# Channel attention on TensorE: the attention weights turned and multiplied with the final weights, then one product over the values

## Chip, cores and metric

The kernel runs on one core of a Trainium2 chip. The metric is the device time of one execution in microseconds; three runs of the kernel before gave a median of 491.94 us (491.89 to 494.11).

## The reference

The input is a batch of 32 images of 96 channels and 16 x 16 pixels. Two layers follow each other: a shifted-window attention with its MLP (layer 0), and a channel attention (layer 1). The change lies in layer 1, whose end is:

```python
Q = _proj(xn, wq_p, bq_p, wq_d, bq_d)
K = _proj(xn, wk_p, bk_p, wk_d, bk_d)
V = _proj(xn, wv_p, bv_p, wv_d, bv_d)
logits = jnp.einsum('bhnc,bhnd->bhcd', K, Q) / alpha[None, :, None, None]
attn = jax.nn.softmax(logits, axis=-1)
out = jnp.einsum('bhnc,bhcd->bhnd', V, attn)
...
return jnp.einsum('bcij,oc->boij', out, w_f) + b_f[None, :, None, None] + xn
```

There are 8 heads of 12 channels each. A head's attention weights are a 12 x 12 matrix, so for one image the weights of all heads are one block matrix over the channels. The output of an image is the final weights times these weights times the values: a chain of three matrices, whose product may be formed from either end.

## The kernel before

Two functions share the work: `window_attention` does layer 0's attention image by image, and `mlp_and_channels` (from L917) does layer 0's MLP, in groups of tokens, and then layer 1, image by image. All matrices are float32. A float32 product appears in the trace as two passes (x2), a transpose by the identity as one.

The last part, from about 340 us to the end, is a loop over images. Its order is written out by hand, one list of calls for each engine (`step`, called by `lap_loop`, L906), and engines meet at semaphores alone. In step t TensorE (L1645) does, in this order:

1. `turn_keys(t)` (L1562): four transposes of queries and keys of image t.
2. `attend(t - 1)` (L1582): attention weights of image t - 1 over its values, 256 columns, into `ps_av`.
3. `queries_and_keys(t + 1)` and, later, `values(t + 1)` (both through `convolve`, L1535): the convolutions, as 24 and 12 small products on tiles of the array 32 columns wide.
4. `gram(t)` (L1570), between the two: 16 products of 12 columns on tiles 32 columns wide.
5. `finalise(t - 1)` (L1589): the final weights over `av_sb`, 256 columns, into `ps_y`.

ScalarE (L1253) copies results from PSUM to SBUF in order: `copy_av(t - 1)` (L1209), `copy_qk(t + 1)` (L1195), the exponent of image t's logits (L1205), a small copy of moments, `copy_v(t + 1)` (L1200) and `pad_x`. VectorE (L1447) copies the turned tokens, normalises a later image, subtracts the peak from the logits, divides by the row sum (`divide`, L1376, which writes `attn`), and adds the residual (`finish`, L1391). SyncE and GpSimd issue the transfers that stack the taps of a later image, and SyncE stores the result.

Values have two buffers, `v_sb[:, par, :]`. `SLOTS` is 4 and is the number of buffers of a padded image; `ROUNDS` is 2, the halves into which the 8 heads are split. `need` is a wait that is left out where its count is not positive. The first copies of `lap_loop`'s body and the last eight are unrolled, the rest is a loop with a register.

Of the kernel before, what the change touches and what calls it, by code (L numbers as in the profile page):

```python
# [20 lines left out]
B, C, H, W = 32, 96, 16, 16  # L21
N = H * W
# [33 lines left out]
def need(engine, semaphore, count):  # L56

    if isinstance(count, int) and count <= 0:
        return
    engine.wait_ge(semaphore, count)  # L60
# [836 lines left out]
SLOTS = 4  # L897
# [19 lines left out]
def mlp_and_channels(nc, ctx, sem, stream, ident, average, w, m, s2, stack_ones, out):  # L917
# [5 lines left out]
    def sb(name, shape, dt=F32):  # L923
        return ctx.enter_context(nc.sbuf_tensor(name, shape, dt))
# [20 lines left out]
    x_pad = sb("x_pad", [C, SLOTS, PADW, PADW])  # L945
    x_stack = sb("x_stack", [128, SLOTS, TILE_HEADS, ROWS])
    qk_sb = sb("qk_sb", [128, ROUNDS, N])
    v_sb = sb("v_sb", [128, 2, N])
    tokens = sb("tokens", [128, 2, ROUNDS, 128])
    logits = sb("logits", [128, ROUNDS, HC])  # L950
    peak = sb("peak3", [128, ROUNDS])
    row_sum = sb("row_sum", [128, ROUNDS])
    recip_sum = sb("recip_sum", [128, ROUNDS])
    attn = sb("attn", [128, ROUNDS, 64])
    av_sb = sb("av_sb", [128, N])
    y_sb = sb("y_sb", [C, 2, N])
    padded_x = nc.dram_tensor("padded_x", (B, C, PADW * PADW), F32, kind="Internal").ap()

# [2 lines left out]
    ps_early = banks[:, 4:8, :]  # L961
    ps_qk = banks[:, 0:2, 0:N]
    ps_v = banks[:, 2, 0:N]
    ps_av = banks[:, 3, 0:N]
    ps_gram = banks[:, 4, 0:ROUNDS * HC].rearrange("p (r d) -> p r d", r=ROUNDS)
    ps_y = banks[0:C, 5, 0:N]
    ps_moments = banks[0:C, 6, 0:2 * B].rearrange("p (t e) -> p t e", e=2)
# [25 lines left out]
    s3 = {n: sem(n + "_3") for n in (  # L993
        "moment_ready", "gained", "normed", "x_padded", "qk_ready", "v_ready", "qk_copied", "v_copied", "tok_ready",
        "tok_copied", "gram_ready", "peak_ready", "shifted", "exp_ready", "sum_ready", "recip_ready",
        "attn_ready", "av_ready", "av_copied", "final_ready", "y_ready")}
    ZEROED = 5
    ONES = 2 * ROUNDS
    OWN = ROUNDS * TILE_HEADS
# [151 lines left out]
    @block.scalar  # L1151
    def _(act):
        def gelu(g, part):
            act.wait_ge(s["hidden_ready"], g * HT + part + 1)
            need(act, s["y_ready"], (g - 1) * SLICES)
            home = ps_early if (g, part) == (0, 1) else ps_hidden
            for r in range(QUARTERS):
                nc.scalar.activation(hidden[:, g % 2, r, part, :], home[:, r, :], ACT.Gelu,  # L1158
                                     bias=fc1_b[:, part:part + 1]).then_inc(s["gelu_ready"], 1)

        def deviation(b):

            first, last = BATCHES[b]
            act.wait_ge(moments_set, MOMENT_OPS * b + 5)
            nc.scalar.activation(log_var[:, first:last], variance[:, first:last], ACT.Ln, scale=0.5,
                                 bias=eps[:, 0:1]).then_inc(log_set, 1)
            act.wait_ge(log_set, b + 1)
            nc.scalar.activation(moments[:, first:last, 0], log_var[:, first:last], ACT.Exp, scale=-0.5).then_inc(rstd_set, 1)

        def await_batch(b):  # L1170

            act.wait_ge(moments_set, MOMENT_OPS * (b + 1))
            act.wait_ge(rstd_set, b + 1)

        def copy_weights(place, kind):

            act.wait_ge(weights_turned, SIDE * (place + 1) + place // 2)
            for half in range(ROUNDS):
                rows, heads = slice(64 * half, 64 * half + STACK), slice(half * HALF_C, (half + 1) * HALF_C)
                at = HC * (half if kind else 1 - half)  # L1180
                nc.scalar.copy(conv_w[rows, kind // 2, :, :, at:at + HC],
                               ps_weights[rows, :, heads].rearrange("p j (h c) -> p j h c", c=HC)).then_inc(weights_copied, 1)

        def take_moment(t, par):

            need(act, s3["normed"], t - 1)
            nc.scalar.copy(moment[:, par, :], moments[:, bass.ds(t, 1), :].rearrange("p a b -> p (a b)")).then_inc(s3["moment_ready"], 1)

        def pad_x(t, lap, slot):

            act.wait_ge(s3["normed"], t + 1)
            act.wait_ge(written[slot], lap * 16)
            nc.scalar.copy(x_pad[:, slot, 1:H + 1, 1:W + 1], grid(stream[:, bass.ds(t * N, N)])).then_inc(s3["x_padded"], 1)

        def copy_qk(t):  # L1195
            act.wait_ge(s3["qk_ready"], t + 1)
            need(act, s3["tok_ready"], t)
            nc.scalar.copy(qk_sb[:, :, :], ps_qk).then_inc(s3["qk_copied"], 1)  # L1198

        def copy_v(t, par):  # L1200
            act.wait_ge(s3["v_ready"], t + 1)
            need(act, s3["av_ready"], t - 1)
            nc.scalar.copy(v_sb[:, par, :], ps_v).then_inc(s3["v_copied"], 1)

        def exponent(t):  # L1205
            act.wait_ge(s3["shifted"], t + 1)
            nc.scalar.activation(logits[:, :, :], logits[:, :, :], ACT.Exp).then_inc(s3["exp_ready"], 1)

        def copy_av(t):  # L1209
            act.wait_ge(s3["av_ready"], t + 1)  # L1210
            need(act, s3["final_ready"], t)
            nc.scalar.copy(av_sb[:, :], ps_av).then_inc(s3["av_copied"], 1)  # L1212

        for g in range(GROUPS - 1):
            later = g > 0
            gelu(g, 0)
            if later:
                for r in range(2):
                    copy_tokens(nc, act, m, s, (g + 1) * QUARTERS + r, tokens_home(r))
            gelu(g, 1)  # L1220
            if later:
                for r in range(2, QUARTERS):
                    copy_tokens(nc, act, m, s, (g + 1) * QUARTERS + r, tokens_home(r))
                nc.scalar.preload_act_table_set("natural_log_exp_and_others")
                token_deviation(nc, act, m, s, g + 1)
                nc.scalar.preload_act_table_set("gelu_and_others")
            gelu(g, 2)
        act.wait_ge(zeroed, ZEROED)
        gelu(3, 0)
        nc.scalar.preload_act_table_set("natural_log_exp_and_others")  # L1230
        deviation(0)
        nc.scalar.preload_act_table_set("gelu_and_others")
        gelu(3, 1)
        copy_weights(0, 1)
        copy_weights(1, 0)
        gelu(3, 2)
        copy_weights(2, 2)
        nc.scalar.copy(final_w[:, :], ps_final).then_inc(weights_copied, 1)
        nc.scalar.preload_act_table_set("natural_log_exp_and_others")
        copy_qk(0)  # L1240
        await_batch(0)
        take_moment(AHEAD, 0)
        copy_v(0, 0)
        deviation(1)

        copy_qk(1)
        exponent(0)
        take_moment(AHEAD + 1, 1)
        copy_v(1, 1)
        pad_x(AHEAD, 1, AHEAD % SLOTS)  # L1250
        await_batch(1)

        def step(t, lap, slot):  # L1253
            copy_av(t - 1)
            if not past(t + 1):
                copy_qk(t + 1)
            exponent(t)
            if not past(t + AHEAD + 1):
                take_moment(t + AHEAD + 1, (slot + AHEAD + 1) % 2)
            if not past(t + 1):  # L1260
                copy_v(t + 1, 1 - slot % 2)
            if not past(t + AHEAD):
                pad_x(t + AHEAD, lap + (slot + AHEAD) // SLOTS, (slot + AHEAD) % SLOTS)
            if is_image(t, 3):
                deviation(2)
                await_batch(2)

        lap_loop(act, step)
        copy_av(B - 1)

    @block.vector
    def _(dve):
# [103 lines left out]
        def divide(t):  # L1376
# [2 lines left out]
            dve.wait_ge(s3["sum_ready"], t + 1)  # L1379
            nc.vector.reciprocal(recip_sum[:, :], row_sum[:, :]).then_inc(s3["recip_ready"], 1)  # L1380
            dve.wait_ge(s3["recip_ready"], t + 1)
            need(dve, s3["av_ready"], t)
            for r in range(ROUNDS):

                nc.vector.scalar_tensor_tensor(  # L1385
# [85 lines left out]
    def _(pe):  # L1471
# [107 lines left out]
                                              tokens[:, n, r, queries:queries + HC], start=(n == 0), stop=(n == 1))  # L1579
            mm.then_inc(s3["gram_ready"], 1)  # L1580

        def attend(t, par):  # L1582
            pe.wait_ge(s3["attn_ready"], (t + 1) * ROUNDS)
            pe.wait_ge(s3["v_copied"], t + 1)
            need(pe, s3["av_copied"], t)
            nc.tensor.matmul(ps_av, attn[:, :, :].rearrange("p r d -> p (r d)"), v_sb[:, par, :], start=True,  # L1586
                             stop=True).then_inc(s3["av_ready"], 1)

        def finalise(t):  # L1589
            pe.wait_ge(s3["av_copied"], t + 1)  # L1590
            need(pe, s3["y_ready"], t)
            nc.tensor.matmul(ps_y, final_w[:, :], av_sb[:, :], start=True, stop=True).then_inc(s3["final_ready"], 1)  # L1592

        up(0, 0)
        up(0, 1)
# [49 lines left out]
        def step(t, lap, slot):  # L1645
            turn_keys(t)
            if not past(t + 1):
                await_taps(t + 1, lap + (slot + 1) // SLOTS, (slot + 1) % SLOTS)
            attend(t - 1, 1 - slot % 2)
            if not past(t + 1):  # L1650
                queries_and_keys(t + 1, (slot + 1) % SLOTS)
            gram(t)
            if is_image(t, 3):
                average_means(2)
            if not past(t + 1):
                values(t + 1, (slot + 1) % SLOTS)
            finalise(t - 1)
            if is_image(t, 3):
                average_spreads(2)

        lap_loop(pe, step)
        attend(B - 1, 1)
        finalise(B - 1)


# [52 lines left out]
```

## Time and profile before

| | before |
|---|---|
| median of three runs | 491.94 us |
| the profiled execution | 491.68 us |
| its span | 490.0 us |
| what lies around the span | 1.68 us |
| TensorE matmuls busy | 475.3 us (97%) |
| weight loads busy | 308.8 us (63%) |
| VectorE busy | 366.1 us (75%) |
| ScalarE busy | 294.8 us (60%) |
| granted clock of TensorE, mean | 0.996 |

The profile comes from one execution. PE is TensorE's matmuls and PEld its weight loads, which can run beside matmuls; DVE is VectorE, ACT is ScalarE. Matmuls are pipelined and their ends are modelled, so the starts of groups say more than their durations. A row of the timeline joins neighbouring instructions of one line: start, time from the first start to the last end, engine, line, what it writes and reads, shape, count, and in brackets the idle time ahead of it and what ended it.

### The profile page before, as it was taken

To read this page: it belongs to the slowest core of one execution; us is meant where nothing else is said; L and a number is where in the kernel's file an instruction comes from. 1 tells how busy PE (TensorE), PEld (TensorE's weight loads), DVE (VectorE), ACT (ScalarE), POOL (GpSimd) and SP (SyncE) were. 2 spreads that over 40 slices of the span, in tenths; PEclk is the share of its full clock that TensorE was granted. 3 is DMA by queue.
4 is the path that set the end of the run, shared out by engine and by line. 5 is a ranking of instruction groups with operands and counts; after the bars stand their busy time and mean duration, and the time that the engine had idled before them with its cause. 6 is when DMAs were issued, how large, how long until landed. Compare 5 with 4: busy or idle time off the path is not lost. (4 is left out here: it accounts for less than half of the span.)

```text
span 490.0 us, 21340 instructions
## 1 busy us (share of the span) xinstructions
PE 475.3 (97%) x8006; PEld 308.8 (63%) x8006; DVE 366.1 (75%) x1013; ACT 294.8 (60%) x757; POOL 186.0 (38%) x230
## 2 busy tenths in 40 slices
PE   8999999999999999999969999999899999999996
PEld 7777777777777777777844344344566666666663
DVE  1599999999999999999873546654966666666553
ACT  2477877787778778877656747642344344444332
POOL 8634343434344434443333012652232333433300
PEclk9999999999999999999999999999999999999998
DMA  4210111111101110110004543475445444444411
GB/s 79 72 36 18 34 33 46 21 33 33 30 19 32 32 27 21 32 32 1 4 7 98 93 105 89 117 181 131 108 111 131 120 107 132 120 111 125 121 41 33
DMA packets 41963, 33.29 MB, mean 68 GB/s; under 512 B 19456, under 2 KB 37760, under 8 KB 41920
## 3 DMA queue, kind: packets, MB, share of 16 engines
q1 hardware_dynamic: 37952, 26.21, 21.5%
q0 software_dynamic: 3968, 6.51, 5.8%
q8 instruction: 28, 0.46, 0.4%
q14 instruction: 15, 0.12, 0.1%
HBM read 19.25 MB, written 7.13 MB: 54 GB/s over the span
## 5 line engine op out<-in xcount | busy, mean ns | idle before, releaser
L379 POOL TENSOR_TENSOR scores<-scores,peak 128x768 f32<-128x768 f32 x64 | 94.2, 1472 | 129.6 <-DVE peak L548 129.6
L1542 PE MATMUL banks<-x_stack,conv_w 40*32 40x256 f32 (+1 forms) x2304 | 97.0, 380 | 0.0
L1017 POOL DMA_DIRECT2D x_stack<-padded_x x96 | 52.3, 548 | 94.6 <-PE banks L1542 56.4
L442 ACT COPY probs_t<-ps_probs 128x768 f32<-128x768 f32 x64 | 51.1, 798 | 40.3 <-PE ps_probs L704 40.2
L1542 PEld LDWEIGHTS banks<-x_stack,conv_w 40*32 40x32 f32 (+1 forms) x2304 | 51.7, 107 | 26.9 <-issue 11.3
L540 DVE TENSOR_TENSOR scores<-ps_scores,bias 128x768 f32<-128x768 f32 x64 | 61.3, 957 | 5.3 <-PE ps_scores L694 3.5
L548 DVE TENSOR_REDUCE peak<-scores 128x12 f32<-128x768 f32 x64 | 61.0, 953 | 2.4
L717 PE MATMUL ps_out<-v_blocks,probs_t 128*64 128x54 f32 x1536 | 57.2, 224 | 0.6 <-ACT out_t L447 0.6
L717 PEld LDWEIGHTS ps_out<-v_blocks,probs_t 128*64 128x64 f32 x1536 | 50.2, 138 | 11.8 <-issue 11.7
L436 ACT ACTIVATE scores<-scores 128x768 f32<-128x768 f32 x64 | 54.2, 847 | 1.5 <-POOL scores L379 1.5
L704 PE MATMUL ps_probs<-ident,scores 128*128 128x128 f32 x384 | 54.3, 277 | 0.0
L694 PE MATMUL ps_scores<-k_blocks,q_sb 32*64 32x256 f32 x768 | 43.1, 399 | 0.9 <-issue 0.9
L704 PEld LDWEIGHTS ps_probs<-ident,scores 128*128 128x128 f32 x384 | 41.5, 140 | 2.8 <-issue 0.8
L527 DVE SCALAR_TENSOR_TENSOR k_blocks<-ps_scores,b_k,head_mask 96x1024 f32<-96x1024 f32 x32 | 40.5, 1267 | 2.8 <-PE ps_scores L672 2.8
L1198 ACT COPY qk_sb<-banks 128x512 f32<-128x512 f32 x32 | 18.8, 587 | 39.0 <-PE banks L1542 39.0
L1158 ACT ACTIVATE hidden<-banks,fc_b_folded 128x512 f32<-128x512 f32 x48 | 29.0, 688 | 21.8 <-PE banks L1498 21.8
L1498 PE MATMUL banks<-normed,fc_sliced 32*128 32x512 f32 x288 | 34.0, 603 | 4.3 <-PEq L148 3.2
L1509 PE MATMUL banks<-hidden,fc 128*32 128x512 f32 x288 | 33.4, 596 | 0.0
L1371 DVE TENSOR_REDUCE peak<-banks 128x2 f32<-128x24 f32 x32 | 5.8, 183 | 36.3 <-PE banks L1578 36.3
L871 POOL TENSOR_TENSOR scaled<-tokens,rstd 128x384 f32<-128x384 f32 x16 | 12.7, 826 | 47.5 <-ACT rstd L863 42.1
L1212 ACT COPY av_sb<-banks 128x256 f32<-128x256 f32 x32 | 11.9, 372 | 27.2 <-PE banks L1586 27.2
L1498 PEld LDWEIGHTS banks<-normed,fc_sliced 32*128 32x128 f32 x288 | 14.3, 184 | 18.7 <-issue 15.8
(146 smaller groups left out, 809.8 us busy)
## 6 DMA issues: line engine op xcount, KB each, us to landing
x_stack<-padded_x SPq DMA_DIRECT2D x96, 54.0 KB
x_stack<-padded_x POOLq DMA_DIRECT2D x96, 54.0 KB, 2.7
padded_x<-x_pad SPq DMA_DIRECT2D x32, 121.5 KB, 2.5
stream<-y_sliced SPq DMA_DIRECT2D x48, 64.0 KB, 2.8
out<-y_sb SPq DMA_DIRECT2D x32, 96.0 KB, 1.9
x_now<-in_x SPq DMA_DIRECT2D x32, 72.0 KB, 1.8
stream<-in_x SPq DMA_DIRECT2D x32, 72.0 KB, 1.9
x_sliced<-stream SPq DMA_DIRECT2D x36, 64.0 KB, 2.0
```

The lines of the kernel that those rows point to most:

```text
L379: nc.gpsimd.tensor_tensor(sc, sc, peak[:, par, p, :].unsqueeze(2).to_broadcast((128, HEADS, WN)), ALU.subtract).then_inc(s["shifted"], 1)
L436: nc.scalar.activation(scores[:, par, p, :], scores[:, par, p, :], ACT.Exp).then_inc(s["probs_ready"], 1)
L442: nc.scalar.copy(probs_t[:, :], ps_turned).then_inc(s["turned_copied"], 1)
L527: nc.vector.scalar_tensor_tensor(out=k_blocks[:, :, :], in0=ps_k.unsqueeze(1).to_broadcast((C, GROUP, N)), scalar=b_k[:, 0:1], in1=head_ma ...
L540: nc.vector.tensor_tensor(scores[:, par, p, :].rearrange("p (g c) -> p g c", g=NG), ps_scores[:, :, 0:GROUP * WN], bias[:, p, :].rearrange ...
L548: nc.vector.tensor_reduce(peak[:, par, p, :], scores[:, par, p, :].rearrange("p (h m) -> p h m", m=WN), AX_X, ALU.max).then_inc(s["peak_re ...
L694: mm = nc.tensor.matmul(ps_scores[64 * w:64 * w + 64, g, 0:GROUP * WN], q, k, start=True, stop=True, skip_group_check=True)
L704: mm = nc.tensor.transpose(ps_turned[:, q * 128:(q + 1) * 128], scores[:, par, p, q * 128:(q + 1) * 128], ident[:, :])
L717: mm = nc.tensor.matmul(ps_out[64 * top:64 * top + 64, 0, q * 2 * VC:(q + 3) * 2 * VC], probs_t[:, q * 128 + 64 * top:q * 128 + 64 * top + ...
L1017: engine.dma_start(x_stack[64 * half + i * HC:64 * half + (i + 1) * HC, slot, :, :], rows).then_inc(landed[slot], 16)
L1498: mm = nc.tensor.matmul(home[:, r, :], fc1[rows, c, part * 128:(part + 1) * 128], normed[rows, c, :], start=(c == 0), stop=(c == SLICES - 1))
L1542: mm = nc.tensor.matmul(home, conv_w[rows, kind, j, k, :], grid(x_stack[rows, slot, k, :], PADW)[:, :, j:j + W], start=(j == 0), stop=(j = ...
```

## The change

For an image, the attention weights are turned on TensorE (`turn_attn`), copied to SBUF, and multiplied with the final weights (`mix`, 96 columns); the result is copied to SBUF, and one product of it with the values (`finalise`, 256 columns) gives the output. The product of the attention weights with the values, and the copy of it, are left out. The values of an image are now needed until the final product, so they have four buffers. The two small results share PSUM bank 3, where the attention over the values was.

```diff
-    v_sb = sb("v_sb", [128, 2, N])
+    v_sb = sb("v_sb", [128, SLOTS, N])
...
-    av_sb = sb("av_sb", [128, N])
+    attn_t = sb("attn_t", [128, 128])
+    mix_sb = sb("mix_sb", [128, C])
...
-    ps_av = banks[:, 3, 0:N]
+    ps_attn_t = banks[:, 3, 0:128]
+    ps_mix = banks[:, 3, 128:128 + C]
...
-        def copy_v(t, par):
+        def copy_v(t, slot):
             act.wait_ge(s3["v_ready"], t + 1)
-            need(act, s3["av_ready"], t - 1)
-            nc.scalar.copy(v_sb[:, par, :], ps_v).then_inc(s3["v_copied"], 1)
+            need(act, s3["final_ready"], t - SLOTS + 1)
+            nc.scalar.copy(v_sb[:, slot, :], ps_v).then_inc(s3["v_copied"], 1)
...
-        def copy_av(t):
-            act.wait_ge(s3["av_ready"], t + 1)
+        def copy_attn(t):
+            act.wait_ge(s3["attn_turned"], t + 1)
+            need(act, s3["mix_ready"], t)
+            nc.scalar.copy(attn_t[:, :], ps_attn_t).then_inc(s3["attn_copied"], 1)
+
+        def copy_mix(t):
+            act.wait_ge(s3["mix_ready"], t + 1)
             need(act, s3["final_ready"], t)
-            nc.scalar.copy(av_sb[:, :], ps_av).then_inc(s3["av_copied"], 1)
+            nc.scalar.copy(mix_sb[:, :], ps_mix).then_inc(s3["mix_copied"], 1)
...
         def step(t, lap, slot):
-            copy_av(t - 1)
+            copy_attn(t - 1)
+            copy_mix(t - 1)
             if not past(t + 1):
                 copy_qk(t + 1)
...
-            need(dve, s3["av_ready"], t)
+            need(dve, s3["attn_turned"], t)
...
-        def attend(t, par):
+        def turn_attn(t):
             pe.wait_ge(s3["attn_ready"], (t + 1) * ROUNDS)
+            need(pe, s3["mix_copied"], t)
+            nc.tensor.transpose(ps_attn_t, attn[:, :, :].rearrange("p r d -> p (r d)"), ident[:, :]).then_inc(s3["attn_turned"], 1)
+
+        def mix(t):
+            pe.wait_ge(s3["attn_copied"], t + 1)
+            nc.tensor.matmul(ps_mix, attn_t[:, :], final_w[:, :], start=True, stop=True).then_inc(s3["mix_ready"], 1)
+
+        def finalise(t, slot):
+            pe.wait_ge(s3["mix_copied"], t + 1)
             pe.wait_ge(s3["v_copied"], t + 1)
-            need(pe, s3["av_copied"], t)
-            nc.tensor.matmul(ps_av, attn[:, :, :].rearrange("p r d -> p (r d)"), v_sb[:, par, :], start=True,
-                             stop=True).then_inc(s3["av_ready"], 1)
-
-        def finalise(t):
-            pe.wait_ge(s3["av_copied"], t + 1)
             need(pe, s3["y_ready"], t)
-            nc.tensor.matmul(ps_y, final_w[:, :], av_sb[:, :], start=True, stop=True).then_inc(s3["final_ready"], 1)
+            nc.tensor.matmul(ps_y, mix_sb[:, :], v_sb[:, slot, :], start=True, stop=True).then_inc(s3["final_ready"], 1)
...
-            attend(t - 1, 1 - slot % 2)
+            turn_attn(t - 1)
             if not past(t + 1):
                 queries_and_keys(t + 1, (slot + 1) % SLOTS)
+            mix(t - 1)
             gram(t)
...
-            finalise(t - 1)
+            finalise(t - 1, (slot - 1) % SLOTS)
```

The calls after the loop change in the same way: `attend` and `finalise` of the last image become `turn_attn`, `mix` and `finalise`, and `copy_av` becomes `copy_attn` and `copy_mix`.

TensorE's list for one step in the kernel before (the names that end in _3 are semaphores of layer 1; L1542 with x23 or x24 is `queries_and_keys`, with x11 `values`):

```order
L1567 MATMUL banks<-ident,qk_sb 128x128 x3
L1586 MATMUL banks<-v_sb,attn 128x256 [waits attn_ready_3,v_copied_3,qk_copied_3,av_copied_3,stacked_pool3,stacked_sp3]
L1542 MATMUL banks<-x_stack,conv_w 32x256 x24
L1578 MATMUL banks<-tokens 32x12 [waits shifted_3,tok_copied_3]
L1578 MATMUL banks<-tokens 32x12 x15
L1542 MATMUL banks<-x_stack,conv_w 32x256 [waits v_copied_3]
L1542 MATMUL banks<-x_stack,conv_w 32x256 x11
L1592 MATMUL banks<-av_sb,final_w 96x256 [waits y_ready_3,av_copied_3]
```

The same step in the changed kernel (its line numbers are its own: L1594 is `turn_attn`, L1598 `mix`, L1604 `finalise`):

```order
L1576 MATMUL banks<-ident,qk_sb 128x128 x3
L1594 MATMUL banks<-ident,attn 128x128 [waits attn_ready_3,qk_copied_3,mix_copied_3,stacked_pool3,stacked_sp3]
L1551 MATMUL banks<-x_stack,conv_w 32x256 x24
L1598 MATMUL banks<-final_w,attn_t 128x96 [waits attn_copied_3]
L1587 MATMUL banks<-tokens 32x12 [waits shifted_3,tok_copied_3]
L1587 MATMUL banks<-tokens 32x12 x15
L1551 MATMUL banks<-x_stack,conv_w 32x256 [waits v_copied_3]
L1551 MATMUL banks<-x_stack,conv_w 32x256 x11
L1604 MATMUL banks<-v_sb,mix_sb 96x256 [waits y_ready_3,v_copied_3,mix_copied_3]
```

At the place of the product of 256 columns there is now a transpose of 128, and a product of 96 columns stands alone between the convolution of queries and keys and the Gram product.

ScalarE's list for one step in the kernel before:

```order
L1212 COPY av_sb<-banks 128x256 [waits final_ready_3,av_ready_3]
L1198 COPY qk_sb<-banks 128x512 [waits tok_ready_3,qk_ready_3]
L1207 ACTIVATE logits<-logits 128x24 [waits shifted_3]
L1187 COPY moment<-moments 96x2 [waits normed_3]
L1203 COPY v_sb<-banks 128x256 [waits av_ready_3,v_ready_3]
L1193 COPY x_pad<-stream 96x16x16 [waits written2,normed_3]
```

And in the changed kernel:

```order
L1214 COPY attn_t<-banks 128x128 [waits mix_ready_3,attn_turned_3]
L1219 COPY mix_sb<-banks 128x96 [waits final_ready_3,mix_ready_3]
L1200 COPY qk_sb<-banks 128x512 [waits tok_ready_3,qk_ready_3]
L1209 ACTIVATE logits<-logits 128x24 [waits shifted_3]
L1189 COPY moment<-moments 96x2 [waits normed_3]
L1205 COPY v_sb<-banks 128x256 [waits final_ready_3,v_ready_3]
L1195 COPY x_pad<-stream 96x16x16 [waits written2,normed_3]
```

One copy of 256 columns has become two, of 128 and 96; the second waits for the product ahead of the Gram product, and the copy of queries and keys stands behind it.

## Rows read from the trace of the kernel before

**Rows 1.** The head of the page: span, then busy us, share and instructions.

```profile
span 490.0 us, 21340 instructions
PE 475.3 (97%) x8006; PEld 308.8 (63%) x8006; DVE 366.1 (75%) x1013; ACT 294.8 (60%) x757; POOL 186.0 (38%) x230
```

**Rows 2.** Busy time in a 30 us stretch, then granted clock, DMA share, GB/s.

```profile
410.00:440.00 30.00, 30.00 (x717) 18.68 (x706) 19.26 (x67) 13.19 (x41) 9.82 (x18) 1.00 0.45 121
```

**Rows 3.** Timeline of TensorE's matmuls, one image and the next Gram product.

```profile
405.04 0.44 PE L1578 MATMUL banks<-tokens 128*32 128x12 f32 x32
...
405.32 1.51 PE L1542 MATMUL banks<-x_stack,conv_w 104*32 104x256 f32 x24
...
406.75 0.67 PE L1592 MATMUL banks<-av_sb,final_w 128*96 128x256 f32 x2
...
407.26 0.60 PE L1567 MATMUL banks<-ident,qk_sb 128*128 128x128 f32 x4
...
407.70 0.60 PE L1586 MATMUL banks<-v_sb,attn 128*128 128x256 f32 x2
...
408.23 1.53 PE L1542 MATMUL banks<-x_stack,conv_w 40*32 40x256 f32 x48
...
409.68 0.44 PE L1578 MATMUL banks<-tokens 128*32 128x12 f32 x32
```

**Rows 4.** Timeline of the weight loads in the same image.

```profile
405.04 0.35 PEld L1578 LDWEIGHTS banks<-tokens 128*32 128x32 f32 x32 [0.41 <-issue]
...
406.75 0.24 PEld L1592 LDWEIGHTS banks<-av_sb,final_w 128*96 128x96 f32 x2 [0.41 <-issue]
...
407.59 0.30 PEld L1586 LDWEIGHTS banks<-v_sb,attn 128*128 128x128 f32 x2
...
408.23 1.04 PEld L1542 LDWEIGHTS banks<-x_stack,conv_w 40*32 40x32 f32 x48 [0.33 <-issue]
```

**Rows 5.** Views of lines 1586 and 1592: loads, ns min/median/max.

```profile
L1586 PEld LDWEIGHTS banks<-v_sb,attn x64: 186/190/192, 339.8 to 485.1; 128*128 128x128 f32 x64
...
L1592 PEld LDWEIGHTS banks<-av_sb,final_w x64: 159/162/280, 343.6 to 486.3; 128*96 128x96 f32 x64
```

**Rows 6.** Timeline of TensorE at image 3: a small product between two groups.

```profile
353.70 0.36 PE L1518 MATMUL banks<-stats,average 96*96 96x32 f32 x2
353.99 1.50 PE L1542 MATMUL banks<-x_stack,conv_w 104*32 104x256 f32 x24
```

**Rows 7.** Timeline of TensorE at images 2 and 3: the Gram product's wait.

```profile
347.60 0.44 PE L1578 MATMUL banks<-tokens 128*32 128x12 f32 x32 [1.01 <-DVE tokens L1366]
...
353.33 0.44 PE L1578 MATMUL banks<-tokens 128*32 128x12 f32 x32 [1.02 <-DVE tokens L1366]
```

**Rows 8.** Timeline of ScalarE and VectorE in the image of rows 3.

```profile
405.22 0.59 ACT L1198 COPY qk_sb<-banks 128x512 f32<-128x512 f32 x1 [1.15 <-PE banks L1542]
...
406.09 0.22 ACT L1207 ACTIVATE logits<-logits 128x24 f32<-128x24 f32 x1 [0.28 <-DVE logits L1373]
...
406.78 0.45 DVE L1385 SCALAR_TENSOR_TENSOR attn<-logits,recip_sum,own_head 128x48 f32<-128x48 f32 x2
...
408.33 0.37 ACT L1212 COPY av_sb<-banks 128x256 f32<-128x256 f32 x1 [0.79 <-PE banks L1586]
```

**Rows 9.** Timeline of the last image, and busy time and clock near the end.

```profile
482.57 0.37 ACT L1212 COPY av_sb<-banks 128x256 f32<-128x256 f32 x1 [1.10 <-PE banks L1586]
...
482.89 0.44 PE L1578 MATMUL banks<-tokens 128*32 128x12 f32 x32 [0.35 <-DVE tokens L1366]
...
485.01 0.70 PE L1586 MATMUL banks<-v_sb,attn 128*128 128x256 f32 x2 [1.08 <-DVE attn L1385]
485.75 0.37 ACT L1212 COPY av_sb<-banks 128x256 f32<-128x256 f32 x1 [1.68 <-PE banks L1586]
...
486.17 1.17 PE L1592 MATMUL banks<-av_sb,final_w 128*96 128x256 f32 x2 [0.46 <-ACT av_sb L1212]
...
486.00:487.00 1.00, 0.83 (x2) 0.40 (x2) 0.00 (x0) 0.12 (x1) 0.00 (x0) 0.51 0.35 98
```

More of the change, by code:

```diff
@@ L995, in mlp_and_channels @@
         "tok_copied", "gram_ready", "peak_ready", "shifted", "exp_ready", "sum_ready", "recip_ready",
-        "attn_ready", "av_ready", "av_copied", "final_ready", "y_ready")}
+        "attn_ready", "attn_turned", "attn_copied", "mix_ready", "mix_copied", "final_ready", "y_ready")}
     ZEROED = 5
@@ L1260, in step @@
             if not past(t + 1):
-                copy_v(t + 1, 1 - slot % 2)
+                copy_v(t + 1, (slot + 1) % SLOTS)
             if not past(t + AHEAD):
@@ L1268, in _ @@
         lap_loop(act, step)
-        copy_av(B - 1)
+        copy_attn(B - 1)
+        copy_mix(B - 1)
     @block.vector
@@ L1661, in _ @@
         lap_loop(pe, step)
-        attend(B - 1, 1)
-        finalise(B - 1)
+        turn_attn(B - 1)
+        mix(B - 1)
+        finalise(B - 1, (B - 1) % SLOTS)
 _INS = ['x', 'L0_conv_qkv_w', 'L0_conv_qkv_b', 'L0_conv_proj_w', 'L0_conv_proj_b', 'L0_conv_rel_bias',
```

## Prediction, made before the changed kernel ran

> **What bounds the kernel now.** I began with the head of the profile's page: TensorE is busy for 97% of a span of 490.0 us [rows 1]. Such a share can hide slack, because ends of matmuls are modelled, so I asked for the busy times of one stretch in the middle of the channel attention, the stage that the change edits: in 30 us TensorE is busy for all 30.00, VectorE for 19.26 and ScalarE for 13.19 [rows 2]. The timeline of one image then shows TensorE's groups without a hole: Gram product at 405.04, values at 405.32, final weights at 406.75, turns of queries and keys at 407.26, attention over the values at 407.70, convolution of the next queries and keys at 408.23, next Gram product at 409.68 [rows 3]. One image is 4.64 us. So an image here costs what TensorE's groups cost from start to start, and the question is what the new groups cost on that scale.
>
> The starts give four prices. A turn of 128 columns is 0.44 / 4 = **0.11 us** [rows 3], so one pass of 256 columns is about 0.21 and one of 96 columns 0.08. Products run as two passes, since each of them shows as x2. A **load** of a stationary matrix is hidden behind the matmul before it when the array keeps its shape. Where the shape changes it is not: the load queue stands idle for 0.33 or 0.41 us and starts only when the group before is over [rows 4]. The final product shows the price: 0.51 us [rows 3] are two passes (0.43) and one open load of 96 columns, 0.08. Its pair of loads says the same: 0.24 together [rows 4], one lasts 0.16 [rows 5], so the second began 0.08 after the first. For 128 columns it is 0.30 together [rows 4] and 0.19 for one [rows 5], so 0.11. And there is a **tail** where a group hands over to another shape: attention over the values takes 0.53 [rows 3], of which two passes are 0.43, so 0.10 is left.
>
> One row tests these prices. At image 3 a small product of 32 columns with a 96-column load stands between two groups of other shapes and takes 353.99 - 353.70 = 0.29 us [rows 6]. My terms give two loads (2 x 0.08, for a pass of 32 columns, 0.03, is too short to hide the second), 0.03 for the last pass and 0.10 of tail: 0.29.
>
> **The change part by part.**
>
> *Attention over the values goes, the turn comes.* 0.53 is removed at its place. The turn there is one pass of 128 columns with its load hidden, for the turns of queries and keys ahead of it have the same shape: 0.11, and the tail of 0.10. Together 0.21, a gain of 0.32 for an image.
>
> *The mix product comes between queries-and-keys and the Gram product.* Both neighbours have other shapes, so this is a new hand-over in each image. No row has it; I bound it. Open load of 128 columns 0.11; first pass 0.08, behind which the second load (0.11) does not fit, so 0.11; second pass 0.08; tail 0.10: **0.40 us**. Lower end 0.34, if loads cost what 96 columns cost (0.08 + 0.08 + 0.08 + 0.10); upper end 0.48, if passes and loads do not overlap at all (0.22 + 0.16 + 0.10). I take 0.40, since the same working meets the 0.29 of the nearest row [rows 6]. The tails of its neighbours are paid already: queries and keys hand over to another shape before and after.
>
> The Trainium skill, "TensorEngine Tiling (Array Packing)", section Tiling Modes, says that a switch of the tiling mode drains TensorE, which speaks against this change. The trace agrees, with the 0.10 us tail; by that rule the sum is mine, and by a switch that cost nothing at the new place it would be 27 x 0.10 = 2.7 us less.
>
> *The final product* keeps its place and shape (a load of 96 columns, two passes of 256): 0.
>
> So an image costs 0.40 - 0.32 = **+0.08 us** more; with unrounded starts I get 0.07 and use that (ends 0.01 and 0.15).
>
> *How many images pay it.* Images 2 and 3 do not: there the Gram product waits 1.01 and 1.02 us for VectorE's copy of the tokens [rows 7], and TensorE's extra work disappears in that hole. Image 3 also leaves its attention to VectorE. From the step of image 4 to that of image 30 TensorE is the bound, so turn and mix count 27 times, 27 x 0.07 = 1.9 to 2.0 us; image 1 adds 0.07, because VectorE's long chain starts from its Gram product.
>
> *ScalarE.* The one 256-column copy (0.37) becomes one of 128 columns and one of 96. Two of its copies, 0.37 for 256 columns and 0.59 for 512 [rows 8], give 0.16 + 0.00084 a column: 0.26 and 0.24. ScalarE has room for 0.13 more. The order matters, though: the copy of the mix now stands ahead of the copy of queries and keys, and that ahead of the exponent on which the next attention depends. The copy of queries and keys starts 0.18 after TensorE passes on to the Gram product (405.22 against 405.04). With the mix there, a copy may start 0.18 after the Gram product's start, take 0.24, and the next 0.59: over at +1.01. The exponent starts at +1.05 today, held by VectorE [rows 8]. It stays there, so I cost this at nothing; the cover is 0.04 us there and, behind it, the gap between the end of the attention weights (406.78 + 0.45) and the load that waits for them (407.59 [rows 4]), 0.36, or 0.31 after the 0.05 that a release takes at the end of the program (a copy over at 486.12, its reader's load at 486.17 [rows 9]). The copy of the turned weights runs under 1.45 us of convolution and is early. The copy of the mix is over some 1.3 us before the final product.
>
> *Queues and buffers.* SyncE and GpSimd issue the same transfers in the same order. Values stay two images longer in four buffers instead of two; the copy into them waits for a final product two images back: 0.
>
> *The end.* In the last image no convolution hides the turned copy. Today the attention of image 30 releases a copy at 482.57 and the Gram product starts at 482.89, held by VectorE [rows 9]. After: the turn's pass ends 0.32 earlier, copy 0.26, release 0.05, mix 0.40: Gram product some 0.1 later. Then the last chain: attention at 485.01, copy at 485.75, final product at 486.17 [rows 9]. After: open load and turn 0.17, release 0.20, copy 0.26, release 0.05, load and passes of the mix 0.30, release 0.20, copy 0.24, release 0.05: final product at 485.01 + 1.47 = 486.48. The granted clock in 486 to 487 is 0.51, the lower level of 1.2 GHz, after TensorE had stood idle behind the copy [rows 9]; if the mix falls under it, its 0.30 doubles. So +0.3 to +0.6, I take 0.5.
>
> **Sum**: 0.07 + 2.0 + 0.1 + 0.5 = +2.7 us, ends 0.8 and 5.0. The profiled execution took 491.68 us, so 494.3; the median of the runs is 491.94, 0.26 above it, so I forecast **494.6 us**. What a measurement can tell from no change is 0.5%, 2.46 us, that is 494.4: my forecast lies on that edge.
>
> **The rivals.**
>
> *Loads run ahead, and it is faster.* If the loads of the mix were taken while the convolution still streams, and its tail hidden, the mix would cost its two passes, 0.16; an image would gain 0.32 - 0.16 = 0.16, 27 images 4.3 us, and with +0.6 at the end the time is about 488.2. It decides at one place, the load queue's idle time ahead of the mix: at 0 it holds. Against it: every change of shape here shows 0.33 to 0.41 us of idle [rows 4]. For it: within one shape loads do run ahead. Chance 0.07. The Trainium skill, "TensorE: Matmul & The Clock Gate", section on what happens when a matmul is issued, says that loads are pulled ahead of running matmuls when row groups do not conflict or the background buffer is the target, which is this case if it held across shapes; the idle rows disagree.
>
> *The mix is at its low end.* At 0.34 an image costs +0.01, and only the end is left: 492.7 to 493.0, no difference to be measured. Chance 0.12.
>
> *The exponent comes late.* ScalarE's longer queue pushes the exponent, VectorE's division and then the turn. Point: the exponent later than +1.05 by more than 0.31; each 0.1 beyond costs 2.7 us, so 497.3. For it: three copies in a row now stand between the mix and the exponent's place, with no slack of their own. Against: the working above. Chance 0.09.
>
> **How the numbers follow.** My case has 0.72; its own range, from the ends of the mix, is 493.4 to 496.0 in the main, and 0.42 of it lies above 494.4, 0.30 below. Slower: 0.42 + 0.09 = 0.51. Same: 0.30 + 0.12 = 0.42. Faster: 0.07. The range, 492.7 to 497.0, takes in both ends of the unknown price (491.94 + 0.8 and + 5.0) and leaves out the faster rival and the far part of the late exponent.
>
> **What would show it.** Right: an image period of about 4.71 us; 0.21 from the turn's start to the convolution; 0.40 from the mix's load to the Gram product's; the load queue idle ahead of both; the exponent still released by VectorE. Wrong: a mix below 0.34 with no idle ahead of it, TensorE waiting for attention weights, or a period under 4.64.

## The result, and the profile after

The changed kernel took 496.95 us (median of six runs, 495.2 to 500.3), 1.0111 times the kernel before, with a 95% interval of 1.0063 to 1.016. The forecast was 494.6, or 1.0054. The direction held, and 496.95 lies just inside the forecast range of 492.7 to 497.0; the increase was about twice the forecast one. The ratio leaves out one slow run of the kernel before (498.98 us). A second set of twelve runs, told below, gave 1.0042 (1.0006 to 1.0078).

The head of the page after:

```profile
span 493.8 us, 21452 instructions
PE 478.3 (97%) x8038; PEld 313.1 (63%) x8038; DVE 366.4 (74%) x1013; ACT 296.2 (60%) x789; POOL 186.0 (38%) x230
```

TensorE has 32 more matmuls (three passes for two in each image) and ScalarE 32 more instructions; the busy shares are those of [rows 1] to within a point.

The timeline of TensorE's matmuls for one image after, to be held against [rows 3]:

```profile
407.54 0.46 PE L1598 MATMUL banks<-final_w,attn_t 128*128 128x96 f32 x2
...
407.93 0.44 PE L1587 MATMUL banks<-tokens 128*32 128x12 f32 x32
...
409.64 0.67 PE L1604 MATMUL banks<-v_sb,mix_sb 128*96 128x256 f32 x2
...
410.15 0.60 PE L1576 MATMUL banks<-ident,qk_sb 128*128 128x128 f32 x4
...
410.59 0.27 PE L1594 MATMUL banks<-ident,attn 128*128 128x128 f32 x1
...
410.79 1.53 PE L1551 MATMUL banks<-x_stack,conv_w 40*32 40x256 f32 x48
...
412.25 0.46 PE L1598 MATMUL banks<-final_w,attn_t 128*128 128x96 f32 x2
```

The mix takes 407.93 - 407.54 = 0.39 us to the Gram product, the turn 410.79 - 410.59 = 0.20. From mix to mix an image is 4.71 us, against 4.64.

The weight loads and ScalarE in the same image:

```profile
407.54 0.30 PEld L1598 LDWEIGHTS banks<-final_w,attn_t 128*128 128x128 f32 x2 [0.41 <-issue]
...
408.04 0.24 ACT L1219 COPY mix_sb<-banks 128x96 f32<-128x96 f32 x1 [1.58 <-PE banks L1598]
408.17 0.59 ACT L1200 COPY qk_sb<-banks 128x512 f32<-128x512 f32 x1
...
408.98 0.22 ACT L1209 ACTIVATE logits<-logits 128x24 f32<-128x24 f32 x1 [0.21 <-DVE logits L1382]
...
410.79 1.04 PEld L1551 LDWEIGHTS banks<-x_stack,conv_w 40*32 40x32 f32 x48 [0.17 <-issue]
```

The load queue idles 0.41 us ahead of the mix, where [rows 4] have 0.33 or 0.41 at a change of shape, and 0.17 ahead of the convolution behind the turn. The exponent starts 408.98 - 407.93 = 1.05 us after the Gram product, where it started before, and VectorE still releases it.

So the image is as forecast. What was not in the forecast shows in the granted clock. Two windows of the profile after (us, busy time and count of TensorE, its loads, VectorE, ScalarE, GpSimd, then granted clock, DMA share, GB/s):

```profile
256.00:259.20 3.20, 3.20 (x20) 1.71 (x16) 0.00 (x0) 0.22 (x1) 3.20 (x6) 0.50 0.29 70
...
354.80:358.20 3.40, 3.40 (x26) 1.55 (x19) 1.88 (x10) 0.98 (x4) 0.00 (x0) 0.50 0.36 86
```

and the second one in the kernel before:

```profile
354.80:358.20 3.40, 3.40 (x66) 2.12 (x62) 2.81 (x12) 1.57 (x5) 0.53 (x1) 1.00 0.33 76
```

At 0.50 TensorE has its lower level, 1.2 GHz: in the second window it started 26 matmuls where it started 66 before. Its timeline gives the price of both falls. After:

```profile
254.59 8.00 PE L1507 MATMUL banks<-normed,fc_sliced 32*128 32x512 f32 x54 [3.21 <-PEq L148]
...
264.25 1.53 PE L887 MATMUL banks<-ident,scaled 128*128 128x128 f32 x12
...
353.98 0.44 PE L1587 MATMUL banks<-tokens 128*32 128x12 f32 x32 [0.96 <-DVE tokens L1375]
...
358.34 0.64 PE L1576 MATMUL banks<-ident,qk_sb 128*128 128x128 f32 x4
```

Before (the Gram product of image 3, at 353.33, is in [rows 7]):

```profile
255.50 6.96 PE L1498 MATMUL banks<-normed,fc_sliced 32*128 32x512 f32 x60 [3.21 <-PEq L148]
...
263.68 1.53 PE L887 MATMUL banks<-ident,scaled 128*128 128x128 f32 x12
...
356.04 0.64 PE L1567 MATMUL banks<-ident,qk_sb 128*128 128x128 f32 x4
```

From the Gram product of image 3 to the turns of image 4 it is 4.36 us after and 2.71 before: 1.65 lost. From the start of the MLP to the transposes behind its first products, in code that the change doesn't touch, it is 9.66 and 8.18: 1.48 lost. Before the first fall TensorE had stood idle for 3.21 us between the window attention and the MLP, as it had in the kernel before, where no fall came; before the second it had waited 0.96 us for VectorE's copy of the tokens, twice. Against these losses, the execution after reached the MLP 0.91 us earlier: at 9 to 15 us some of its first products took less, six of them 0.59 us (L637) where they took 1.01 before. The two profiled executions differ by 495.54 - 491.68 = 3.86 us; less 1.48 and 1.65, and with the 0.91, that leaves 1.6 for the change itself.

### The profile page after: what moved, and what is told of

It is laid out like the page before. It is cut to its first block and busy times, and to the rows that moved or that the text cites. A ratio compares the mean times of both kernels' runs of the same rounds, so it can differ in the third digit from the quotient of the medians.

```text
span 493.8 us, 21452 instructions
## 1 busy us (share of the span) xinstructions
PE 478.3 (97%) x8038; PEld 313.1 (63%) x8038; DVE 366.4 (74%) x1013; ACT 296.2 (60%) x789; POOL 186.0 (38%) x230
## 5 line engine op out<-in xcount | busy, mean ns | idle before, releaser
L1551 PE MATMUL banks<-x_stack,conv_w 40*32 40x256 f32 (+1 forms) x2304 | 98.2, 382 | 0.0
L1507 PE MATMUL banks<-normed,fc_sliced 32*128 32x512 f32 x288 | 35.4, 628 | 4.3 <-PEq L148 3.2
L1219 ACT COPY mix_sb<-banks 128x96 f32<-128x96 f32 x32 | 7.6, 238 | 47.7 <-PE banks L1598 47.7
L1205 ACT COPY v_sb<-banks 128x256 f32<-128x256 f32 x32 | 11.9, 372 | 24.0 <-PE banks L1551 24.0
```

The costliest lines, as they stand in the source:

```text
L1507: mm = nc.tensor.matmul(home[:, r, :], fc1[rows, c, part * 128:(part + 1) * 128], normed[rows, c, :], start=(c == 0), stop=(c == SLICES - 1))
L1551: mm = nc.tensor.matmul(home, conv_w[rows, kind, j, k, :], grid(x_stack[rows, slot, k, :], PADW)[:, :, j:j + W], start=(j == 0), stop=(j = ...
```

## The experiments

There were two theories of the excess. Either the change provokes the fall of the clock at image 3, or such falls come and go in any kernel and the first six runs met more of them.

**The kernel before, again, unedited.**

> The kernel before, unedited, to see how its time and mean granted clock spread from run to run. Theory 'drop by the change' (the change costs 0.067 us an image, and besides makes TensorE's clock fall to 1.2 GHz for some 3.4 us at image 3, where it lost 1.6 us): mean clock near 0.996 in all runs, times 490 to 492 us. Rival 'drops in every kernel' (such falls come and go whatever this stage does): mean clock between 0.974 and 0.996 as in the runs of the change, times from 490 to 498 us that go with it, and the profile shows falls too.

493.2 us over twelve runs (491.75 to 496.16), mean clocks from 0.978 to 0.990. Its profile shows no fall between 20 and 486 us, and the times rise as the clock goes down: 491.75 at 0.989, 496.16 at 0.978. Both theories had a point: there was no fall in the stage that the change edits, but a spread of 4.4 us with no edit at all. The 35 runs of the kernel before beside it had a median of 493.47, 1.5 us over the 491.94 on which the forecast was built.

This profiled execution's 491.75 us at a mean clock of 0.989 stand beside the 491.68 at 0.996 behind the forecast. The two start alike; 9 to 15 us, and twelve products there, first in the forecast's execution, then in this one:

```profile
9.00:15.00 6.00, 6.00 (x28) 5.03 (x29) 1.44 (x9) 0.72 (x3) 5.58 (x11) 1.00 0.42 91
11.18 2.13 PE L109 MATMUL ps_probs<-blank 96*96 96x96 f32 x12
```

```profile
9.00:15.00 6.00, 6.00 (x27) 5.03 (x28) 1.44 (x9) 0.66 (x2) 5.59 (x11) 0.50 0.42 91
11.26 2.13 PE L109 MATMUL ps_probs<-blank 96*96 96x96 f32 x12
```

The products take the same 2.13 us, but the row of the granted clock says 1.00 in one and 0.50 in the other. So a mean clock can leave out a stretch at the program's start, and 0.996 marks no faster execution than 0.989 here.

**The changed kernel, again, unedited.**

> The changed kernel, unedited, a second time, beside the kernel before on the same chip. Theory 'drops in every kernel': its mean clock spreads as that of the kernel before did in its second set (median 0.986), its span at a clock of 0.987 is 493.5 us, some 2.0 us over the kernel before, and its median time is 494.5 to 496, a ratio of 1.003 to 1.006. Theory 'drop by the change': its median clock stays at 0.982 as in the first six runs, the ratio at 1.009 to 1.012, and the profile shows the fall at image 3 again.

495.06 us (492.17 to 500.33), ratio 1.0042 (1.0006 to 1.0078). The median clock is 0.9875, not 0.982, and its profile has no fall at image 3 or at 256 us. The rival's numbers came out. Its own runs give the price of the clock: 492.21 us at 0.995 and 498.86 at 0.978, that is 3.9 us for 0.01. The 0.0055 between the median clocks of the two sets is worth 2.1 us, and their medians differ by 1.9. By that price the first set's excess is the clock's. But the profile is of one of the six runs at 0.991 or more; the other six, from 496.40 us up and at 0.984 or less, left none, so a fall at image 3 isn't excluded in them.

Since neither of these two profiles has a fall between 20 us and the end of the loop, they show the change by itself. TensorE's timeline where the bound stretch begins and ends, kernel before, then changed:

```profile
356.63 0.69 PE L1586 MATMUL banks<-v_sb,attn 128*128 128x256 f32 x2
...
482.01 0.60 PE L1586 MATMUL banks<-v_sb,attn 128*128 128x256 f32 x2
```

```profile
356.74 0.32 PE L1594 MATMUL banks<-ident,attn 128*128 128x128 f32 x1
...
483.87 0.27 PE L1594 MATMUL banks<-ident,attn 128*128 128x128 f32 x1
```

27 images take 127.13 us for 125.38: +1.75, 0.065 an image. The two executions also start alike (the first scores of the window attention at 16.75 and 16.71 us), so their whole difference, 493.53 - 491.75 = 1.78 us, is the change.

**Filling the hole at image 3.**

```diff
         def mix(t):
             pe.wait_ge(s3["attn_copied"], t + 1)
+            if is_image(t, 1) or is_image(t, 2):
+                for _ in range(4):
+                    nc.tensor.matmul(ps_mix, attn_t[:, :], final_w[:, :], start=True, stop=True)
             nc.tensor.matmul(ps_mix, attn_t[:, :], final_w[:, :], start=True, stop=True).then_inc(s3["mix_ready"], 1)
```

> The changed kernel, but the mix products of images 1 and 2 are made five times instead of once, in the 0.96 us for which the Gram product waits for VectorE. Theory 'drop by the change': TensorE works through the hole, the fall of the clock at image 3 goes, 1.6 us less than the change (495.3 or less), the hole shrinks to nearly nothing. Rival 'drops in every kernel': time within 0.5 us of the change at the same mean clock, falls at image 3 or not.

494.69 us, median clock 0.9875: within 0.4 us of the changed kernel's second set at the same clock. The hole was filled, the profile has no fall at image 3, and the median won nothing. Both theories allow this median (495.3 or less by one, within 0.5 us by the other), so by itself it doesn't refute the theory that the open hole can bring a fall: nothing above 497.38 us is among these twelve, while three of the second set took 498.07 to 498.86. The runs with another stretch filled, at the end of this section, speak against it: there the hole at image 3 is open, and 23 of 24 runs lie from 490.85 to 494.07. Among the profiles of all kernels the fall at image 3 was seen once; whether the hole brings it in executions that fell earlier stays open.

**The mix beside the final product.**

```diff
             if not past(t + 1):
                 queries_and_keys(t + 1, (slot + 1) % SLOTS)
-            mix(t - 1)
             gram(t)
...
-            finalise(t - 1, (slot - 1) % SLOTS)
+            mix(t - 1)
+            if not is_image(t, 1):
+                finalise(t - 2, (slot - 2) % SLOTS, slot % 2)
```

`mix_sb` gets two buffers, `copy_mix` moves behind `copy_v`, and the last addition and the store come one image later.

> The changed kernel with the mix product moved from between the convolution and the Gram product to just ahead of the final product, which comes one image later, so that full-array groups stand together and the hand-over of the mix (open load and tail) is gone. Theory 'hand-over': the image period falls from 4.707 to 4.54 us (4.64 - 0.32 + 0.22), 27 images give 4.5 us less than the change and some 2.2 less than before at the same clock, 489 to 490 us. Rival 'small products and their copies cost as such': period 4.70 or more, 495 us or more.

490.1 us, ratio 0.9945 (0.9914 to 0.9975). The timeline of its matmuls:

```profile
424.66 0.46 PE L1602 MATMUL banks<-final_w,attn_t 128*128 128x96 f32 x2
424.96 0.60 PE L1608 MATMUL banks<-v_sb,mix_sb 128*96 128x256 f32 x2
425.39 0.60 PE L1580 MATMUL banks<-ident,qk_sb 128*128 128x128 f32 x4
425.83 0.27 PE L1598 MATMUL banks<-ident,attn 128*128 128x128 f32 x1
426.03 1.53 PE L1555 MATMUL banks<-x_stack,conv_w 40*32 40x256 f32 x48
...
429.20 0.46 PE L1602 MATMUL banks<-final_w,attn_t 128*128 128x96 f32 x2
```

and its loads:

```profile
424.66 0.30 PEld L1602 LDWEIGHTS banks<-final_w,attn_t 128*128 128x128 f32 x2 [0.41 <-issue]
424.88 0.25 PEld L1608 LDWEIGHTS banks<-v_sb,mix_sb 128*96 128x96 f32 x2
```

The period is 4.54 us, as expected. The mix keeps its passes and its copy, but it has the array's shape in common with the final product behind it: that one's loads start without idle time, the mix has no tail of its own, and mix and final product together take 425.39 - 424.66 = 0.73 us where they took 0.39 + 0.51. So the mix costs 0.22 us here and 0.39 there, of which 0.16 are its passes in either place: the place decided, not the small product and its copies as such.

**A lone product in the kernel before.** It is made of the identity and the final weights, its result goes to a free part of a PSUM bank, and nobody reads it.

```diff
                 queries_and_keys(t + 1, (slot + 1) % SLOTS)
+            nc.tensor.matmul(ps_lone, ident[:, :], final_w[:, :], start=True, stop=True)
             gram(t)
```

> The kernel before with a lone product of 96 columns, whose result nobody reads, between the convolution of queries and keys and the Gram product; all else stays. Theory 'hand-over': 0.39 us more in each image that TensorE bounds, an image period of 5.03 us against 4.64, some 11 us in all. Rival, that the change's 0.39 holds a wait for ScalarE's copy: 0.3 or less, a period of 4.94 or less.

503.61 us in a single run. Its matmuls:

```profile
420.87 0.46 PE L1653 MATMUL banks<-final_w,ident 128*128 128x96 f32 x2
421.26 0.44 PE L1579 MATMUL banks<-tokens 128*32 128x12 f32 x32
...
425.90 0.46 PE L1653 MATMUL banks<-final_w,ident 128*128 128x96 f32 x2
```

0.39 us to the Gram product and a period of 5.03. This product waits for no copy, so the 0.39 holds no wait for ScalarE.

**Spreading VectorE's statistics**, with the change and without it.

```diff
-            if is_image(t, 1):
-                take_moments(2, 0, 8)
-            if is_image(t, 2):
-                take_moments(3, 0, 8)
+            if isinstance(t, int) and 1 <= t <= 7:
+                for j in ((0, 1, 2), (3, 4, 5), (6, 7), (8, 9), (10, 11), (12, 13), (14, 15))[t - 1]:
+                    take_moments(2 + j // 8, j % 8, j % 8 + 1)
```

The averages, the deviation and the wait for them move from image 3 to 8, and eleven steps are unrolled instead of three.

> The changed kernel with VectorE's 16 image statistics spread over the steps 1 to 7 instead of 8 each in steps 1 and 2, and the averages taken at step 8 instead of 3 (the first 11 steps are written out instead of 3), so that the Gram products of images 2 and 3 no longer wait. Theory 'drop by the change': both holes (2 x 0.96 us) and the fall at image 3 (1.6 us) go, 3.5 us less than the change. Rival 'drops in every kernel': 1.9 us less at the same clock, the clock falls elsewhere as often as before.

> The kernel before with the image statistics spread over seven steps. Theory, the holes are worth their 1.0 us each and nothing in them depends on the change: some 2.0 to 2.2 us less than the kernel before at the same clock, ratio 0.995 to 0.997. Rival, that the hole mattered only with the change: ratio 1.000.

With the change: 493.1 us at a median clock of 0.987, so 2.0 us less than the second set's 495.06 at 0.9875, which is what the two waits of 0.96 us held. Without it: 491.93 us, ratio 0.994 (0.9907 to 0.9973), at a median clock of 0.984; by that ratio 3.0 us, with 1.3 to 4.6 in the interval. So the holes are worth about 2 us with the change, and the run without it agrees within its interval.

> The changed kernel with both edits: the mix product just ahead of the final product, and the image statistics spread over seven steps. If the two gains add (hand-over 4.9 us, measured as 488.55 against 493.5 at a clock of 0.987; holes 2.2, measured as 491.3 against 493.5), the span at that clock is 486.3, the time 488 and the ratio to the kernel before 0.988 to 0.991. Rival, that VectorE's later final step leaves no room for the statistics: span 488 or more.

Spread and beside the final product together: 488.76 us over six runs, ratio 0.9906 (0.9871 to 0.994). By the median, 490.1 - 488.76 = 1.3 us of the 2.0 came through.

**Filling the idle time between the stages.** Six of the ten profiles up to here, of kernels with the change and without it, show the clock fall between 253 and 262 us, right behind the 3.2 us in which TensorE waits for the next part to begin.

```diff
         led_image_loop(pe, step)
+        pe.wait_ge(fold_copied, SLICES)
+        fill(nc, free, blank[:, :], 12)
```

> The changed kernel with 12 products of 96 columns that nobody reads at the end of TensorE's first part, in the 3.2 us for which it stands idle between the window attention and the MLP; the rest stays. Theory 'idle, then the fall': the clock's fall that six of the ten profiles show between 253 and 262 us goes where TensorE works through this stretch; the idle time there shrinks to about 1 us, the profile shows no fall there, the median clock rises from 0.9875 to 0.990 or more and the median time falls by 0.5 to 1.5 us (493.6 to 494.6). Rival, that the fall there has another cause: profile and median as the unedited kernel's, 495.1.

492.31 us for 495.06, with a median clock of 0.994, and no fall behind the filling in the profile; the gain was larger than expected. Against the kernel before, run beside it, the ratio is 0.997 (0.9939 to 1.0001). TensorE's timeline, and the window in this kernel and in the first profile of the change:

```profile
251.15 2.20 PE L109 MATMUL ps_probs<-blank 96*96 96x96 f32 x24
254.52 7.82 PE L1509 MATMUL banks<-normed,fc_sliced 32*128 32x512 f32 x68 [1.18 <-PEq L148]
```

```profile
253.00:262.00 9.00, 7.83 (x73) 4.00 (x75) 0.53 (x2) 5.27 (x9) 6.17 (x10) 1.00 0.30 74
```

```profile
253.00:262.00 9.00, 7.42 (x54) 3.78 (x58) 0.60 (x2) 3.58 (x6) 6.17 (x10) 0.81 0.28 68
```

The idle time is down to 1.18 us. All four profiles of kernels with this filling keep the upper level there. One of the twelve runs still took 499.88 at 0.975; no profile shows where its clock fell.

> The kernel before with TensorE's idle time between the stages filled (12 products that nobody reads), to be compared with the changed kernel under the same filling, run beside it. Theory 'idle, then the fall': median clock 0.992 or more, and 490 to 491 us against some 493 without the filling; the changed kernel under the filling lies 1.7 to 2.3 us above it, a ratio of 1.0035 to 1.0047. Rival, that the change itself lowers the clock: the two differ by more than 3 us and their median clocks by more than 0.003.

> The changed kernel with the same filling, a second time: 492.3 us, 1.7 to 2.3 us above the kernel before with the filling if 0.067 us an image is all that the change costs; more than 3 us above it if the change lowers the clock.

With the filling, the kernel before took 491.64 us (median clock 0.9915) and the changed one 493.46 (0.9945), on one chip: 1.82 us, a ratio of 1.0037. The difference is the one expected, and the clock is not lower with the change. The kernel before missed its 490 to 491 us: against the same kernel unfilled, run beside it, the ratio is 0.9983 (0.9958 to 1.0008), so no gain is shown by that measure. What differs is the upper end: 10 of the 23 unfilled runs took 493 to 495 us, and none of the 12 filled ones more than 492.25.

The changed kernel lay 1.2 us over its first filled set. The two profiles place this at the program's start, where the same twelve products took, first set and second:

```profile
10.31 1.18 PE L109 MATMUL ps_probs<-blank 96*96 96x96 f32 x12
```

```profile
11.22 2.13 PE L109 MATMUL ps_probs<-blank 96*96 96x96 f32 x12
```

The first scores of the window attention then start at 15.63 and at 16.78 us, 1.15 apart, and the spans differ by 1.1. So, by these two profiles, some 1.2 of the 2.75 us that the first filled set gained over 495.06 came from the start and not from the filling. The two profiled executions of e11 and e12 start alike, at 16.82 and 16.78, and differ by 493.58 - 491.89 = 1.69 us. The row of the granted clock again doesn't tell: over 9 to 15 us it says 1.00 in the second set, as in the forecast's execution.

> The changed kernel with all three edits: the mix product ahead of the final product, the statistics spread, the idle time between the stages filled. If the gains add, 487 to 488.5 us, a ratio to the kernel before of 0.988 to 0.991; if the filling is worth nothing, 488.8 as without it.

All three edits on the changed kernel: 486.18 us over six runs (484.35 to 486.47), ratio 0.9835 (0.9802 to 0.9868). This version beats both kernels, and by more than the sum foreseen.

## Why the prediction was right or wrong

- **The image: right.** Turn 0.20 (forecast 0.21), mix 0.39 (0.40), period 4.71 (4.71). The mechanism held with its sizes: the price of a hand-over between shapes, read from the idle time ahead of the loads and from a small product at image 3 [rows 6], carried over to a place that had none; the lone product confirmed it. Had the rival of loads that run ahead held, the load queue would not have idled 0.41 us ahead of the mix.
- **How many images: right.** 27 images give 1.75 (forecast 1.9 to 2.0), image 1 gives 0.07. Images 2 and 3 hide it in VectorE's hole, with waits of 0.96 us for 1.01 and 1.02 [rows 7].
- **ScalarE: right.** The exponent stays at +1.05 and is released by VectorE; the copy of queries and keys ends before it.
- **The end: wrong by 0.7.** "+0.3 to +0.6, I take 0.5" was about -0.2: at the loop's last product (482.01 and 483.87) the change lies 1.86 us behind, and the spans of these two executions differ by 1.7. The chain got longer, but in the first profile after it ran at the upper level throughout:

```profile
489.04 0.33 PE L1594 MATMUL banks<-ident,attn 128*128 128x128 f32 x1 [1.05 <-DVE attn L1394]
489.40 0.27 ACT L1214 COPY attn_t<-banks 128x128 f32<-128x128 f32 x1 [1.31 <-PE banks L1594]
...
489.72 0.46 PE L1598 MATMUL banks<-final_w,attn_t 128*128 128x96 f32 x2 [0.36 <-ACT attn_t L1214]
490.22 0.24 ACT L1219 COPY mix_sb<-banks 128x96 f32<-128x96 f32 x1 [0.55 <-PE banks L1598]
...
490.51 0.67 PE L1604 MATMUL banks<-v_sb,mix_sb 128*96 128x256 f32 x2 [0.33 <-ACT mix_sb L1219]
```

Its window (columns as above):

```profile
486.00:491.30 5.30, 3.09 (x43) 1.57 (x41) 2.41 (x10) 1.23 (x5) 0.00 (x0) 1.00 0.13 37
```

From the turn to the final product it is 1.47 us, exactly as worked out, for 1.16 before. But the final product takes 0.67 where it took 1.17 at the lower level [rows 9], and that gives the difference back.
- **The sum: wrong, because it has no term for the clock ahead of the last image.** The step is "0.07 + 2.0 + 0.1 + 0.5 = +2.7 us", set on "the profiled execution took 491.68 us, so 494.3; the median of the runs is 491.94". The clock enters it only under the end; a fall anywhere else was put at nothing without a reason, although three runs from 491.89 to 494.11 stood in front of me. The base itself came out, at 491.91 in the runs beside the result, but it is the time of an execution with no fall behind its first 20 us: the kernel's larger sets have medians of 492.52 to 494.13. In place of nothing the runs showed 1.48 + 1.65 us of falls in the first profile of the change, and a median clock of 0.982 in its first six runs; by 3.9 us for 0.01 that accounts for the 1.9 us to the second set. The terms that the sum does have come to less than 2.7 together: 1.78 us between two executions with a like start and no fall (491.75 and 493.53), and 1.69 with the filling. The larger sets give 2.2 (495.06 against 492.89). So without the falls the increase is smaller than forecast, and with those of the first six runs larger. Why these six had so many stays open.
- **The page on the tiling mode.** One hand-over fewer between shapes, with the loads behind it hidden, gives 0.17 us back: a period of 4.54 us for 4.71. The Trainium skill, "TensorEngine Tiling (Array Packing)", section Tiling Modes, says that a switch of the tiling mode drains TensorE; the trace agrees with these 0.17 us. In these traces loads ran ahead of a running product between groups of the full array, as those of the final product do behind the mix, and the queue idled 0.17 to 0.41 us ahead of the mix and of the convolution behind the turn. The Trainium skill, "TensorE: Matmul & The Clock Gate", Part 2: What happens when you issue a matmul, states that loads are pulled ahead of running products where row groups don't conflict or the background buffer is the target; the trace has such loads within one shape, and none at the changes of shape shown here.

## What to carry to other kernels

Where TensorE is the bound, count hand-overs between array shapes as well as columns: a small product between two groups of another shape costs its open load and its tail (0.39 us here, of which 0.16 are its passes), and the same product beside a group of its own shape costs 0.22. Before a forecast of half a per cent is built on one profiled execution, ask how the granted clock spreads from run to run; here 0.01 of it was worth 3.9 us, more than the change. Compare the durations of like products too, since the clock's row can miss a stretch at the start. Where TensorE stands idle between stages, products that nobody reads can be worth their place: here they took away most of the slow upper end of the runs, though for the kernel before no gain in the mean was shown.

## What was not expected of the hardware

The clock fell to 1.2 GHz right behind 3.2 us of idle TensorE in six of ten profiles, and in none of the four where 2.2 us of that time were filled. The same code with the same idle time fell or didn't from run to run. A granted clock of 1.00 can stand over products that take as long as at 0.50: twelve of them, at 11 us, took 2.13 us in two executions of the kernel before, in one at 1.00 and in the other at 0.50. Where the falls of the runs with clocks of 0.974 to 0.980 lie stays open, since one execution in each set was profiled; and why the first six runs of the change had more of them was not settled beyond the second set of twelve, which did not repeat their median.
